# A graph layer on one core: pair loops written out, and all transfers of adj started from one queue

## The reference

```
def reference(x, adj, L0_gnn_weight):      # x 8192 x 256, adj 8192 x 8192, weight 256 x 256, all float32
    bw = sign(weight)
    ba = maximum(sign(x), 0.0)
    xw = ba @ bw.T                          # 8192 x 256
    out = adj @ xw                          # the large product
    return layernorm(x + relu(out), axis=-1)
```

## Time and profile before

| what | value |
|---|---|
| median of 3 runs | 1066.31 us (1064.25 to 1069.69) |
| span of the profiled execution | 1064.2 us |
| PE busy | 993.5 us, 93% |
| DVE, POOL, ACT busy | 858.2, 840.3, 605.2 us |
| moved by DMA | 294.36 MB, mean 277 GB/s |
| moved by SP's queue (q1) | 168.06 MB |
| moved by ScalarE's queue (q10) | 125.84 MB |

### The profile page before, as it was taken

How to read it: one execution, slowest core, us unless ns; L and a number is a source line. 1 busy time by engine, 2 the same in 40 slices (tenths; PEclk the granted TensorE clock), 3 DMA queues, 4 the chain that set the end, 5 groups by cost and what they waited for, 6 DMA issues and landing times.

```text
span 1064.2 us, 15065 instructions
## 1 busy us (share of the span) xinstructions
PE 993.5 (93%) x4484; PEld 812.8 (76%) x4484; DVE 858.2 (81%) x881; ACT 605.2 (57%) x647; POOL 840.3 (79%) x361
## 2 busy tenths in 40 slices
PE   5578699999998999899998999899998999999996
PEld 4356578888877888788886888778886888888885
DVE  4656489898959989598886989599895989799893
ACT  3345366666546656466565665466564665566562
POOL 0346489899868988599896998599885998889893
PEclk9889899999999999999999999989999999999999
DMA  9999999999998999899998999999998999999961
GB/s 216 226 223 224 228 286 320 302 332 317 308 315 241 292 324 282 250 295 311 299 297 250 300 313 294 290 236 289 327 284 253 300 306 299 300 290 297 309 198 39
DMA packets 313166, 294.36 MB, mean 277 GB/s; under 512 B 9760, under 2 KB 313120, under 8 KB 313120
## 3 DMA queue, kind: packets, MB, share of 16 engines
q1 hardware_dynamic: 186400, 168.06, 62.3%
q10 hardware_dynamic: 126720, 125.84, 42.3%
HBM read 285.47 MB, written 8.39 MB: 276 GB/s over the span
## 4 chain that ended last, share of the span: by engine, by line
PE 44%; POOL 26%; issue 12%; SPq 9%; DMA 4%; DVE 3%; ACT 1%; POOLq 0%; ACTq 0%
PE ps L619 44%; POOL lo L299 26%; SPq L217 7%; DMA raw<-in_adj_dram 4%; SPq L205 2%; DVE turned L450 1%; DVE lo L456 1%; PE ps L644 1%; DVE ps L450 0%; ACT hi L326 0%; DVE relu L414 0%; DVE stats L464 0%; POOLq L298 0%; SPq L195 0%; ACT rows L344 0%
## 5 line engine op out<-in xcount | busy, mean ns | idle before, releaser
L299 POOL TENSOR_TENSOR lo<-turned,hi 128x1024 fp32r<-128x1024 f32 x352 | 839.2, 2413 | 207.1 <-ACT hi L326 203.9
L619 PE MATMUL ps<-hi,xw 128*128 128x512 f32 x2048 | 810.0, 396 | 31.8 <-DVE lo L456 27.1
L619 PE MATMUL ps<-lo,xw 128*128 128x512 f32 x2048 | 804.8, 393 | 0.0
L326 ACT ACTIVATE hi<-turned 128x1024 fp32r<-128x1024 f32 x352 | 373.4, 1061 | 281.4 <-DVE turned L450 161.7
L619 PEld LDWEIGHTS ps<-hi,xw 128*128 128x128 f32 x2048 | 389.6, 190 | 120.0 <-DVE lo L456 24.9
L619 PEld LDWEIGHTS ps<-lo,xw 128*128 128x128 f32 x2048 | 389.4, 190 | 80.4
L450 DVE STREAM_TRANSPOSE turned<-raw 128x1024 f32<-128x1024 f32 x352 | 426.1, 1218 | 22.3 <-DMA raw<-in_adj_dram 22.3
L456 DVE TENSOR_TENSOR lo<-ps,hi 128x1024 fp32r<-128x1024 f32 x160 | 194.8, 1217 | 128.1 <-ACT hi L326 127.5
L326 ACT ACTIVATE hi<-ps 128x1024 fp32r<-128x1024 f32 x160 | 164.1, 1025 | 134.4 <-issue 58.9
L450 DVE STREAM_TRANSPOSE ps<-raw 128x1024 f32<-128x1024 f32 x160 | 195.1, 1219 | 18.6 <-DMA raw<-in_adj_dram 18.6
L344 ACT ACTIVATE rows<-rows,shift,rstd 128x256 f32<-128x256 f32 x62 | 36.4, 588 | 0.0
(11 more groups left out here) (23 smaller groups left out, 47.8 us busy)
## 6 DMA issues: line engine op xcount, KB each, us to landing
raw<-in_adj_dram ACTq DMA_DIRECT2D x240, 512.0 KB, 10.4
raw<-in_adj_dram SPq DMA_DIRECT2D x240, 512.0 KB, 9.0
raw<-in_adj_dram SPq DMA_DIRECT2D x64, 256.0 KB, 7.4
x_sb<-in_x_dram SPq DMA_DIRECT2D x32, 256.0 KB, 8.1
rows<-in_x_dram SPq DMA_DIRECT2D x16, 512.0 KB, 8.8
out_dram<-rows SPq DMA_DIRECT2D x15, 512.0 KB, 13.7
out_dram<-rows SPq DMA_DIRECT2D x2, 256.0 KB, 2.3
rows<-in_L_gnn_weight_dram SPq DMA_DIRECT2D x1, 256.0 KB, 3.7
```

The lines of the kernel that those rows point to most:

```text
L299: pool.tensor_tensor(lo[:, s], turned[:, t], hi[:, s].bitcast(f32), ALU.subtract).then_inc(p_los_made, 1)
L326: act.activation(hi[:, s], src, ACT.Copy).then_inc(his_made, 1)
L619: return pe.matmul(acc[h][a], xw[:, step, a * P:(a + 1) * P], part[:, s, k * MB:(k + 1) * MB], start=(step == 0 and part is hi), stop=(ste ...
```

## The change

All five loops over pairs are written out by the program that builds the kernel, so the engines get straight code for 8 pairs. `load_chunk` on SP starts all four quadrants of each chunk, in the order 0, 2, 1, 3. ScalarE's `load_chunk_after` is gone, and with it all transfers that ScalarE started. Waits, buffers and the arithmetic are as before.

```
 def load_chunk(q, h, c):
     n = (q * 2 + h) * CH + c
     sp.wait_ge(units_turned, (n - SLOTS + 1) * UPC)
-    start_chunk(sp, q, h, c, LOWER)
+    start_chunk(sp, q, h, c, IN_TURNS)
...
     load_block(0, 1)
-    with sp.Fori(1, PAIRS) as q:
+    for q in range(1, PAIRS):
         for h in range(2):
             load_block(q, h)
...
-    pair(0)
-    with pool.Fori(1, PAIRS) as q:
+    for q in range(PAIRS):
         pair(q)
...
-    def load_chunk_after(q, n):
-
-        later, c = divmod(n // UPC + SLOTS, 2 * CH)
-        in_block_0 = known_met(q) and n // UPC + SLOTS < CH
-        beyond_the_end = isinstance(q, int) and q + later >= PAIRS
-        if n % UPC == UPC - 1 and not in_block_0 and not beyond_the_end:
-            start_chunk(act, q + later, c // CH, c % CH, UPPER)
...
             make_hi(q, n)
-            load_chunk_after(q, n)
...
-    pair(0)
-    with act.Fori(1, PAIRS - 1) as q:
+    for q in range(PAIRS):
         pair(q)
-
-    pair(PAIRS - 1)
...
-    pair(0)
-    with dve.Fori(1, PAIRS) as q:
+    for q in range(PAIRS):
         pair(q)
...
-    pair(0)
-    with pe.Fori(1, PAIRS) as q:
+    for q in range(PAIRS):
         pair(q)
```

## The result

The changed kernel takes 1290.49 us, the median of 4 runs (1266.68 to 1307.83), against 1067.2 us for the kernel before (1064.25 to 1069.69, 4 runs). The ratio is 1.195 with a 95% interval of 1.187 to 1.204; it goes by the executions within 1.5% of the fastest of their kernel, and the spread of 3% is a subject of the experiments. The profiled execution took 1297.77 us with a span of 1296.0.

A forecast was written before the change was run, and what follows sets the result against it. PE's matmuls bound the kernel before; one queue's transfers would bound the changed one. Block 0 114, adj 1128, rows 50, code 3 and end 21 sum to 1316 us of span, plus 2 gives 1318; range 1200 to 1410.

The forecast's parts named there:

- The rate of adj, 223 GB/s, range 206 to 249: Blocks 1 to 15: one queue brings 251.7 MB of adj at 223 GB/s, 1128 us; chance 0.77 for 206 to 249.
- The model of the overlap: Adj transfers: each change of side saves 0.24 us, giving 213 GB/s; if overlap grows with the transfer, 235.
- Block 0, 114 us: Kernel start: block 0, x and the weights, 25.4 MB at 223 GB/s, take 114 us, as before.
- The end, 21 us: After the last chunk lands: transpose, copy, POOL's three units, the last unit's matmuls and the old ending, together 21 us.
- SP's waits, 0 us: SP's two waits per block, for finished rows and the store's landing, cost 0; without cover by transfers, 70 us.
- ScalarE's starts and the five stalls: Removing ScalarE's 240 transfer starts gains nothing; removing its five pair-end stalls gains 31 us, only while PE decides.
- PE keeps pace: PE's matmuls need 1.81 us per unit, 1.97 at clock 0.92, of the 2.36 its data takes, so PE stays covered.
- Code fetching, 3 us: Written-out loops: 0.8 MB more instructions to fetch cost 3 us of transfer time, with 0 and 8 as ends.
- The signs: Profile after: flat 220 to 235 GB/s, PE near 75%, DVE waiting for raw, landing well above 9.0 us, packets 75 to 92 ns.
- The queue makes no difference: Rival: adj rate stays near 303 GB/s or above, PE decides, five stalls go, 1035 us; chance 0.08.
- The DMA engines drift apart: Rival: during adj transfers some DMA engines stand on one side, others on the other; 270 GB/s, 1122 us; chance 0.10.
- One side's rate, 194: Rival: adj moves at only one side's 194 GB/s, with no help from the order, 1487 us; chance 0.04.

The follow-up runs named there:

- splitting in four: Changed kernel with each 512 KB transfer of adj cut into four of 128 KB, in turns over the quadrants: 1122.48 us, ratio 1.053.
- the loops alone: Kernel before with all loops over pairs written out, both queues loading adj as before: 1035.16 us, ratio 0.971.
- the queue-only kernel: Kernel before, loops kept, but SP starts all transfers of adj and ScalarE none: 1149.72 us (1103.27 to 1224.06); repeated, 1306.2 us.

## Why the prediction was right

The main step, that one queue going over the sides carries some 223 GB/s and that this decides, held: 24% more time was forecast, and the median rose by 21%. By its own terms, against the profiled execution's 1296.0 us:

- **The rate of adj, 223 GB/s, range 206 to 249.** SP starts the last transfer of adj at 1261.8 us, and it lands 11.5 us later (the only start from 1262 to 1264 us, with its time to landing):

```profile
raw<-in_adj_dram SPq DMA_DIRECT2D x1, 512.0 KB, 11.5
```

From the landing of block 0's last part at 113.9 us to this one at 1273.3 the kernel moved 251.7 + 14.7 MB of adj and rows and some code in 1159 us, 230 GB/s. My terms for that were 1128 + 50 + 3 = 1181 us, 22 too many, and this is nearly all that the forecast was off. The usual stretches have 223 to 229; the faster one, 316 GB/s from 228 to 264 us, makes up part of the rest.
- **The model of the overlap.** A fixed 0.24 us for each change of side would have given 213 for 512 KB, and the other end 235. The measured 223 to 229 of the usual stretches lies between them, and splitting in four fits: the saving grows with size, but less than in proportion. That one fixed rate could describe these transfers was wrong: the same ones went at 340 GB/s in another execution. That the middle of two ends met the average so well is in part luck.
- **Block 0, 114 us.** Its last part landed at 113.9.
- **The end, 21 us.** It took 1296.0 - 1273.3 = 22.7, right within 2 us, but by another path than the one summed. The chain's end shows it (start us, us, what):

```profile
1251.87 14.49 DMA raw<-in_adj_dram
...
1266.39 1.25 DVE turned L437
...
1268.80 4.79 POOL lo L299 x2
...
1273.63 13.01 PE ps L605 x56
```

The landing at 1266.4 is that of the last chunk but one. From 1273.6 on PE worked without a pause through 56 matmuls, the three units of that chunk that were left and the four of the last. So PE set the pace there with 13.0 us, where I had POOL's three units and the last unit's 8 matmuls behind them.

- **SP's waits, 0 us.** Right as a sum: SP waited 20.6 us for 15 stores with no gap in the DMA share. The reason given was partly wrong. Not three chunks stood ahead of a store: at one start every 2.2 us and 10.2 us to landing, four or five transfers of 512 KB are on their way at a time.
- **ScalarE's starts and the five stalls.** Right: nothing for the former while transfers decide, and the stalls were worth 31 us as worked out, shown by the loops alone at 1035. The cause lay in ScalarE's loop only. One detail was misread: behind the stall at 443 us 8 matmuls went at 0.43 us, not 13, at a granted clock of 0.51, the lower level; they cost 1.6 us and not 2.6.
- **PE keeps pace.** Right as a condition, but it was busy for 84% and not near 75%: 2.0 us for a unit (200.38 us for 793 matmuls from 1000 to 1240 us) where I had 1.81 to 1.97, of the 2.4 that a unit then took.
- **Code fetching, 3 us.** Too small to be seen: ScalarE's loop alone and all loops written out took the same time. The two queues of kind "instruction" moved 0.77 MB against 0.45 before, so 0.3 MB more and not 0.8.
- **The signs.** DVE's waits for adj, the packet time of 77 ns and the end of ScalarE's idle time by "issue" came as named. The row of GB/s wasn't flat at 220 to 235, and landing took 10.2 us against 9.0, not well above it. A stretch over 260 GB/s with one queue was named as a sign of being wrong, and there was one, 36 us at 316. It doesn't touch the sides, but it does touch the fixed rate that the sum was built on.
- **The rivals.** "The queue makes no difference" fell with the transfers over all partitions and with two queues on one side. The Trainium skill's sentence behind it ("DMA: Bandwidth & Descriptors", section "Issuing engines are not separate DMA queues") holds in a narrower sense: 356 GB/s from one queue agrees that the number of queues isn't what counts. That starting transfers on several engines saves only the sequencer's time isn't so here: two queues, each on its own side, gave 347 GB/s where one in turns gave 235, and the measurement decides. "The DMA engines drift apart", at 1122 us with a chance of 0.10, has a time that did occur, whatever its cause: runs of the queue-only kernel took 1103, 1110 and 1122 us, outside the forecast's range, while all 12 runs of the changed kernel (1222 to 1326) lie inside it. I had no reason in the sum for that difference. "One side's rate, 194" fell; even the order 0, 1, 2, 3 was at 216 to 236 GB/s.

What stays open is what brings the high rate of one queue about and what ends it, beyond that most of the abrupt changes fall on passes of rows. The records don't say which DMA engine moved a packet, so engines that are out of step, some writing one half of the partitions while others write the other, is an explanation that fits and isn't shown.

## What to carry to other kernels

Read the rate of a transfer stream in stretches where it has the DMA engines to itself, and compare it for the partitions that it writes, before moving it to another queue: two queues may be fast only because each keeps to its half of the partitions. Where a transfer could cover all 128 partitions, one queue was enough here. A change that joins a gain (31 us of a loop's stalls) with a loss (some 250 us of transfer rate) is best measured in halves: here the gain of 31 us is there only while PE decides.

## What the runs showed of the hardware

- Transfers over 32 partitions at a time from one queue: mostly 223 to 229 GB/s in turns of 512 KB (250 in the stretch of 200 us that holds the fast part), 267 to 279 in turns of 128 KB, against 356 over all 128 partitions; two queues on the same side 226, and 241 on average from 200 to 1200 us.
- The same single queue held 340 GB/s for 43 us in one execution and 231 behind the next pass of rows, and whole executions of one kernel differed by 20% (1110 to 1326 us) on one chip. With transfers over all 128 partitions the spread was 0.2%.
- At a pair's end ScalarE's loop cost 10.8 to 11.4 us of its time; four other engines looped at the same places and cost nothing that shows in the total (1035.95 against 1035.16 us).
- The granted TensorE clock stayed at 0.96 to 1.00 of the 2.4 GHz level in the stretches after the first 119 us (0.94 there), though PE was busy for only 84% of the time and waited again and again.
